# Layer 0 of a two-layer graph network: gathered rows in another column order, two harmonics weighted in one product, the parts summed by one reduce and one addition

## What is computed

```python
xs = x[:, :MUL_S]
xv = x[:, MUL_S:].reshape(n, MUL_V, 3)
...
out_s = (jnp.einsum('eu,uo->eo', xs_e * es[:, None], W_ss) / np.sqrt(MUL_S) + jnp.einsum('eud,ed,uo->eo', xv_e, ev, W_vv) * ISQ3 / np.sqrt(MUL_V)) * ISQ2
out_v = (jnp.einsum('eu,ed,uv->evd', xs_e, ev, W_sv) * ISQ3 / np.sqrt(MUL_S) + jnp.einsum('eud,e,uv->evd', xv_e, es, W_vs) * ISQ3 / np.sqrt(MUL_V)) * ISQ2
messages = jnp.concatenate([out_s, out_v.reshape(-1, 3 * MUL_V)], axis=1)
scale = jax.nn.sigmoid(edge_scalars @ W_rad.T + b_rad)
messages = messages * scale
agg = jax.ops.segment_sum(messages, dst, num_segments=n)
```

## Time and profile before

| | us |
|---|---|
| median of three runs | 4380.39 |
| profiled execution | 4373.24 |
| its span | 4371.4 |
| DVE busy | 3896.0 |
| PE busy | 3899.9 |
| POOL busy | 3139.9 |
| ACT busy | 2657.9 |

### The profile page before, as it was taken

The page is one execution under the profiler, slowest core; times in us unless marked ns, Lnnn a source line. Parts: engine busy times, 40 slices in busy tenths (PEclk is TensorE's granted clock), DMA queues, the critical chain, the costliest instruction groups (busy, mean ns, idle before and its releaser), DMA issues.

```text
span 4371.4 us, 64745 instructions
## 1 busy us (share of the span) xinstructions
PE 3899.9 (89%) x14024; PEld 2512.9 (57%) x14025; DVE 3896.0 (89%) x8569; ACT 2657.9 (61%) x8217; POOL 3139.9 (72%) x3268
## 2 busy tenths in 40 slices
PE   7899999989999998899878898899888898898887
PEld 5566666656666666666655555555555555555555
DVE  4999999999999999999768888998888998889987
ACT  5666666666666666666555566666656666566664
POOL 4777777777777777777457777777777777777771
PEclk7655555565555556655789999999999999999999
DMA  9666666666666666666333333333333333333331
GB/s 292 192 194 192 191 193 192 192 194 191 191 194 192 191 192 191 191 195 192 112 94 102 100 100 102 104 102 103 104 102 102 103 102 104 103 102 104 103 103 54
DMA packets 245745, 640.05 MB, mean 146 GB/s; under 512 B 57085, under 2 KB 95423, under 8 KB 245611
## 3 DMA queue, kind: packets, MB, share of 16 engines
q0 software_dynamic: 181136, 556.56, 46.4%
q1 hardware_dynamic: 64576, 83.11, 6.1%
HBM read 618.56 MB, written 20.88 MB: 146 GB/s over the span
## 4 chain that ended last, share of the span: by engine, by line
DVE 51%; PE 18%; issue 15%; DVEq 6%; DMA 4%; ACT 3%; POOL 2%; POOLq 0%; ACTq 0%; SPq 0%
PE ps L998 11%; DVE work L694 10%; DVE onehot L738 10%; DVE work L668 6%; DVE arena L746 4%; DVE work L718 3%; DVE work L661 3%; PE ps L975 3%; DMA arena<-table,srcs 3%; DVE work L681 2%; DVE work L715 2%; ACT work L480 2%; DVEq L803 2%; DVE acc L746 2%; POOL arena L383 2%
## 5 line engine op out<-in xcount | busy, mean ns | idle before, releaser
L383 POOL DMA_INDIRECT arena<-table,srcs x1596 | 1543.3, 967 | 486.4 <-issue 434.0
L383 POOL DMA_INDIRECT work<-table,srcs x1596 | 1526.1, 956 | 496.0 <-issue 479.8
L998 PE MATMUL ps<-work,onehot 128*128 128x384 f32 x3608 | 1310.8, 510 | 224.4 <-DVE work L725 129.2
L480 ACT ACTIVATE work<-arena,harm 128x160 f32<-128x160 f32 (+1 forms) x3224 | 985.4, 388 | 417.8 <-DMA arena<-table,srcs 400.5
L998 PE MATMUL ps<-arena,onehot 128*128 128x161 f32 x3608 | 1025.4, 461 | 183.2 <-DVE arena L704 156.2
L998 PEld LDWEIGHTS ps<-arena,onehot 128*128 128x128 f32 x3608 | 875.4, 305 | 501.6 <-issue 433.6
L480 ACT ACTIVATE work<-work,harm 128x96 f32<-128x96 f32 (+1 forms) x3224 | 1071.4, 415 | 131.1 <-DMA work<-table,srcs 73.7
L998 PEld LDWEIGHTS ps<-work,onehot 128*128 128x128 f32 x3608 | 670.9, 195 | 773.9 <-issue 325.4
L975 PE MATMUL ps<-wrad,escal 49*128 49x320 f32 x1612 | 899.8, 703 | 0.0
L738 DVE SCALAR_TENSOR_TENSOR onehot<-ps,bases,dst_sh 128x512 f32<-128x512 f32 x902 | 669.9, 743 | 14.6 <-DVE acc L746 7.3
L694 DVE TENSOR_REDUCE work<-work 128x256 f32<-128x768 f32 (+1 forms) x806 | 654.0, 850 | 1.5 <-ACT ps L508 1.0
(11 more groups left out here) (130 smaller groups left out, 2240.1 us busy)
## 6 DMA issues: line engine op xcount, KB each, us to landing
escal<-in_escal SPq DMA_DIRECT2D x404, 98.0 KB
arena<-table,srcs POOLq DMA_INDIRECT x1596, 3.5
work<-table,srcs POOLq DMA_INDIRECT x1596
table<-work SPq DMA_DIRECT2D x49, 224.0 KB, 5.9
dst_sh<-in_dst_sh SPq DMA_DIRECT2D x52, 160.0 KB, 3.2
table<-work SPq DMA_DIRECT2D x7, 784.0 KB, 4.0
acc<-in_xd SPq DMA_DIRECT2D x1, 3920.0 KB, 22.3
arena<-in_xd SPq DMA_DIRECT2D x7, 560.0 KB, 4.2
```

The lines of the kernel that those rows point to most:

```text
L383: pool.indirect_dma_start(out=rows[:, j, t, :], out_offset=None, in_=table, in_offset=bass.IndirectOffsetOnAxis(ap=of[:, j, t:t + 1], axis ...
L480: last = nc.scalar.activation(u[:, t, to:to + c1 - c0], r[:, t, c0:c1], ACT.Copy, scale=harm[:, j, at:at + 1])
L998: last = mm(bank(to)[:, 0:(MSG0, MSG1)[l]], onehot[:, b, t, :], m[:, j % 2, t, :], start=t == 0, stop=t == TPS - 1)
```

## The change

The table's columns, and with them the rows, are laid out anew, so that the two harmonics that DVE weights stand next to each other and all four parts of the scalars lie at the same distance in `weighted0`, as do the three components of the vectors. The rows of x are put in another order on the host for it. In the edge loop of layer 0:

- ACT weights columns 288 to 448 with harmonic 3 and 192 to 288 with harmonic 0, in eight instructions as before; the semaphore `s_whead` is gone.
- DVE copies the harmonics of a whole round into PSUM (`harm0`, bank 7), once a round, and makes one product for harmonics 1 and 2 over 128x768 elements, with the harmonics from PSUM, in place of the product of 384 elements and the four passes. It waits for the rows (`s_rows`) and not for ACT.
- It sums the four parts of the scalars in one reduce over 1024 elements, and the two parts of the vectors in one addition of 384 elements, in place of two reduces over 768 and 512 elements.

```diff
@@ weight_rows0
-                weight(u, r, 3, 96, 256, 128, j % PAIR).then_inc(s_whead, 1)
-                weight(u, r, 0, 256, 352, 288).then_inc(s_wtd[0], 1)
+                weight(u, r, 3, 288, 448, 64, j % PAIR)
+                weight(u, r, 0, 192, 288, 224).then_inc(s_wtd[0], 1)
@@ weight_by_one
                 if l == 0:
-                    dve.wait_ge(s_whead, s + 1)
+                    if j == 0:
+                        nc.vector.tensor_copy(harm0, of_round(i, slice(0, SLOTS), slice(TPS, 5 * TPS)).bitcast(f32)).then_inc(s_harmp[0], 1)
+                        dve.wait_ge(s_harmp[0], i + 1)
+                    dve.wait_ge(s_rows[0][j], (i + 1) * 16 * TPS)
                     u, r = weighted0[:, j % DEEP0, :, :], rows0[:, j, :, :]
-                    nc.vector.tensor_tensor(u[:, :, 384:480], r[:, :, 352:448], by(1), ALU.mult)
-                    for t in range(TPS):
-                        if t == 1:
-                            dve.wait_ge(s_add[0], s + 1)
-                        if t == TPS - 1 and not opens:
-                            dve.wait_ge(s_agg[0], s + 1)
-                        to = u[:, t, 128:224]
-                        last = nc.vector.scalar_tensor_tensor(to, r[:, t, 0:96], harm[:, j, 4 * t + 2:4 * t + 3], to,
-                                                              ALU.mult, ALU.add)
-                    last.then_inc(s_wone[0], 1)
+                    nc.vector.tensor_tensor(u[:, :, 320:512].rearrange("p t (k c) -> p t k c", k=2),
+                                            r[:, :, 0:192].rearrange("p t (k c) -> p t k c", k=2),
+                                            bc(harm0[:, j, :].rearrange("p (t k) -> p t k", k=4)[:, :, 1:3], 3, [P, TPS, 2, 96]),
+                                            ALU.mult).then_inc(s_wone[0], 1)
+                    if not opens:
+                        dve.wait_ge(s_agg[0], s + 1)
@@ messages0
-                summed(u[:, :, 0:MS], 160, 3)
+                dve.wait_ge(s_wtd[0], s + 1)
+                parts = u[:, :, 160:544].rearrange("p t (k c) -> p t k c", k=4)
+                nc.vector.tensor_reduce(u[:, :, 0:MS], parts[:, :, :, 0:MS].rearrange("p t k c -> p t c k"), AX.X, ALU.add)
                 dve.wait_ge(s_act[0], s + 1)
-                summed(u[:, :, MS:2 * MS], 224, 2).then_inc(s_part[0], 1)
+                vectors = u[:, :, MS:DIM].rearrange("p t (k c) -> p t k c", k=3)
+                nc.vector.tensor_tensor(vectors, vectors, u[:, :, 224:512].rearrange("p t (k c) -> p t k c", k=3)[:, :, :, 0:MV],
+                                        ALU.add).then_inc(s_part[0], 1)
@@ SCALED0: ACT scales w0a in two pieces in place of three; block.tensor: the second product of the table goes to other columns
-                mm(p[:, 32:128], x1[:, of_tile], w0b[:], start=False, stop=True).then_inc(s_tmm, 1)
+                mm(p[:, 224:320], x1[:, of_tile], w0b[:], start=False, stop=True).then_inc(s_tmm, 1)
```

More of the change, by code:

```diff
@@ L156, in mk_gnn_resnorm_d2_gnn_r8_694f30_kernel @@
         hps = bank(7)
+        harm0 = hps[:, 0:4 * TPS * SLOTS].rearrange("p (j c) -> p j c", j=SLOTS)
         half = [two_to_a_bank(2 * b, 224)[:, :, 192:] for b in range(2)]
@@ L438, in _ @@
             act.wait_ge(s_w0, 32)
-            for w, c in SCALED0[:3]:
+            for w, c in SCALED0[:2]:
                 nc.scalar.activation(w, w, ACT.Copy, scale=c).then_inc(s_w0scaled, 1)
@@ L616, in _ @@
                     dve.wait_ge(s_w0, 32)
-                    for w, c in SCALED0[3:]:
+                    for w, c in SCALED0[2:]:
                         nc.vector.tensor_scalar(w, w, c, None, ALU.mult).then_inc(s_w0scaled, 1)
@@ L1199 @@
     by_component = np.concatenate([s_of, *v_of])
+    v_of_kept = [MS + MV * d + np.arange(MV) for d in range(3)]
     xd = placed(NODES_PAD, DIM, (0, 0, x[:, by_component]))
@@ L1223 @@
     ins = {
-        "xT": xd.T, "xd": xd,
+        "xT": xd.T[np.concatenate([s_of, *(v_of_kept[d] for d in (1, 2, 0))])], "xd": xd,
         "srcs": np.concatenate([by_supertile(src, 0).transpose(1, 0, 2), np.zeros((P, SLOTS, TPS), src.dtype)], axis=1),
```

12 lines of the change are left out of this document (3 added, 9 removed).

## The result

| | before | changed |
|---|---|---|
| median of the runs, us | 4381.05 (4379.35 to 4384.94, 4 runs) | 4487.9 (4477.52 to 4491.06, 4 runs) |
| ratio, 95% interval | | 1.0239 (1.0227 to 1.0251) |
| span of the profiled execution, us | 4371.4 | 4489.2 |
| last gather of layer 0 starts at, us | 2107.7 | 2218.6 |

The forecast was 4363 us with a range of 4348 to 4390; 4487.9 lies 98 us above that range. The whole loss is in the edge loop of layer 0: its last gather starts 110.9 us later. From its first to its last gather, layer 1 takes 2036 us (2041 before).

What follows compares the result with a forecast made beforehand. It took POOL's gathers to pace layer 0, with DVE nearly tied. Gather surplus -32 us, new holds +16 and layer end -1 turned the profiled 4373.24 into 4356, or 4363 against the runs' median 4380.39; range 4348 to 4390.

Steps and rivals of the forecast that it cites:

- the price of the reduce: DVE, layer 0 edge loop: one reduce over 1024 elements taken at 1.29 us, 1.21 after overlap.
- a reduce well over 1.3 us: One of the listed signs that would show the prediction wrong, for the new DVE reduce in layer 0.
- fourth rival: No relief: with a big reduce of 1.7 us DVE keeps its 40.2 us, the layer its time; 4380 us, chance 0.07.
- the prediction's own sum for DVE: Layer 0, eight supertiles after the change: 8 x 4.29 + 2 x 1.14 + 1.1 = 37.7 us, below POOL's 40.06.
- The upper end of the range: 4390 us, taking in the blind-places rival (4375, chance 0.21) and part of the PE rival (4402, chance 0.06).
- POOL's bound and what DVE gives back: Layer 0: POOL's gathers set the pace; of DVE's 0.38 us saved a supertile only POOL's surplus returns, 32 us.
- the last message: End of layer 0: its start after the last gather falls from 10.74 to 9.7 us, - 1 us.
- the product's price and the addition's: DVE, layer 0: product of 128x768 at 0.87 us to the next start; addition of 384 elements 0.55, 0.59 with its wait.
- a gather which has started doesn't hold DVE: Layer 0: the addition runs its usual time inside a gather; rival, a lock in both directions, 4409 us, chance 0.01.
- The rival without stretches at full clock: PE at 1.2 GHz throughout needs 2072 us in layer 0, + 22 us; 4402 us, chance 0.06.
- the round: DVE, once a round in layer 0: 0.89 us of loop plus 0.25 for copy and wait, 1.14 us.
- the addition's place: Layer 0: the new addition falls mostly clear of gather starts, holding them 0.04 us a supertile, 16 us in all.

Runs made afterwards that it cites:

- four adjacent: Changed kernel, but the reduce sums four numbers lying side by side, not the four parts of one output, so its sums are others: 4350.63 us, ratio 0.9943.
- three parts: Changed kernel with the reduce over three of the four scalar parts, one left out of the sum: 4350.66 us, ratio 0.9928.
- three in PSUM, then one: Changed kernel with a reduce of three scalar parts into PSUM and an addition of the fourth in place of the four-part reduce: 4363.66 us, ratio 0.995.
- three in SBUF, then one: Changed kernel with a reduce of three scalar parts into SBUF and an addition of the fourth in place of the four-part reduce: 4376.89 us, ratio 0.9984.
- two additions: Changed kernel with the four scalar parts summed by additions of 512 and 256 elements, all inputs in SBUF, in place of the reduce: 4397.6 us, ratio 1.0037.
- two and three parts: Changed kernel with a three-part reduce, one part left out, and ahead of it an unread two-part reduce into PSUM: 4387.9 us, ratio 1.0006.
- three parts twice: Changed kernel with a three-part reduce, one part left out, and ahead of it an unread three-part reduce into PSUM: 4520.63 us, ratio 1.0327.

## Why the prediction was wrong, step by step

The second column adds the durations of what stands in the place of the scalar sum. In the kernel before it is both reduces, which do the vectors too; all others have the addition of 0.55 us for these beside it.

| kernel | sums, us | gathers in 200 to 1900 us | eight supertiles, us | mean gather there, ns | time, us | ratio |
|---|---|---|---|---|---|---|
| before | 1.70 | 1337 | 40.69 | 967 | 4381.1 | 1 |
| changed | 1.91 | 1263 | 43.07 | 952 | 4487.9 | 1.0239 |
| four adjacent | 1.21 | 1347 | 40.39 | 958 | 4350.6 | 0.9943 |
| three parts | 1.02 | 1351 | 40.27 | 954 | 4350.7 | 0.9928 |
| three in PSUM, then one | 1.46 | 1341 | 40.57 | 963 | 4363.7 | 0.995 |
| three in SBUF, then one | 1.45 | 1335 | 40.75 | 969 | 4376.9 | 0.9984 |
| two additions | 1.11 | 1318 | 41.27 | 986 | 4397.6 | 1.0037 |
| two and three parts | 1.72 | 1329 | 40.93 | 974 | 4387.9 | 1.0006 |
| three parts twice | 2.05 | 1243 | 43.77 | 945 | 4520.6 | 1.0327 |

- **The step that failed is the price of the reduce.** The prediction took 768 elements at 1.020 us and 512 at 0.681 and carried the line on to 1024, with ends of 1.28 and 1.36. Both rows are of sums whose parts are few enough; the third point of the line didn't exist. It took 1.906. The rows of before couldn't show this, but they did show that both known forms were other forms (two parts, three parts), and the bound should have been as wide as that. The prediction named "a reduce well over 1.3 us" as the sign of a mistake, and its fourth rival started from 1.7 us; it had 0.07.
- **What followed from it.** With 1.83 from start to start in place of 1.21, and 1.34 a round in place of 1.14, the prediction's own sum for DVE reads 37.7 + 8 x 0.62 + 2 x 0.20 = 43.06 us for eight supertiles. Measured: 43.07. The model of the two engines was right, and fed with the right price it gives the loss.
- **The rival that had a long reduce was mispriced, too.** It said that with a reduce of 1.7 us DVE would keep its 40.2 us and the layer its time, 4380. By the prediction's own sum a reduce of 1.7 us gives 37.7 + 8 x 0.41 = 41.0 us of DVE, already more than POOL's 40.7; 40.2 belongs to a reduce of 1.6. The kernel with 4.62 us a supertile, what a single reduce of 1.906 - (4.89 - 4.62) = 1.64 us would give, was at a ratio of 1.0006. There is no plateau behind that point. From there on each further us per eight supertiles costs 48 to 50, and the step to 1.9 is 102 us. The upper end of the range was set from cases in which DVE at most kept its time.
- **Right: POOL's bound and what DVE gives back.** With a reduce of 1.21 us (1.29 was assumed) the kernel takes 0.9943 of the time of before, the forecast was 0.9960 (4363 of 4380.39), just above the interval (0.9926 to 0.9959). The last gather moved by 13.3 us where 16 were predicted, and the last message followed it after 10.41 us (10.74 before) where 9.7 were. The rest of the gain lies elsewhere (see the end of this section), so the agreement of the total is in part luck.
- **Right: the product's price and the addition's**, and, in the main, that a gather which has started doesn't hold DVE: in no kernel did the additions take more than their usual time in the mean (543 to 554 ns for the 384 elements). Only those that started within some 0.05 us of a gather's start, on either side, were longer, by up to 0.08 us.
- **PE was not the bound.** The rival without stretches at full clock did not come in: the granted clock of the changed layer 0 was 0.56 (0.58 before), and DVE never waited for PE.
- **A size that was off: the round.** Copy, wait and loop cost 1.34 us where 1.14 stood (1.46 in the kernels that have one instruction more for the scalar sum); the copy was taken at 0.25 with its wait and needs 0.37 to the product's start. It is 0.4 us in eight supertiles; with the reduce at 1.29 us DVE would still have been below POOL's 40.06.
- **Partly right: the addition's place.** Between 600 and 1200 us it held 15 gathers of 120 supertiles in the kernel with three parts (DVE early, the predicted place mostly clear), but 40 of 119 with adjacent numbers and 42 of 118 with the sum in PSUM. At nearly the price that I had assumed, the place was nearly blind, at 0.06 us a supertile (7.0 us for 119) and not 0.04.

What stays open: the last gather of the four-adjacent kernel explains 13 us of its gain; the median is 27 below that of before. The profiled executions are 24 apart, and 9 of these lie in layer 1 (2031.9 us from first to last gather, 2041.0 before), whose instructions the change doesn't touch. The traces say where: POOL's few pauses there cost 9.6 us before and 4.4 in this kernel, and its gathers, 956 and 954 ns in the mean, make the other 4. Over the eleven kernels with the change layer 1 took 2027.9 to 2039.2 us. With one trace of each, chance isn't ruled out, and why the pauses differ isn't shown.

## What to carry to other kernels

An instruction's price can be carried along a line only within its form: before merging sums, ask how the addresses of one output lie, and price a new form of access by a form as far away as the doubt is, here the factor of 1.6 between 1.91 and 1.22 us. Where two engines run at nearly the same period, a saving on the one that is not the bound is worth only what it was costing the other, while every us that takes it past the meeting point is paid in full: the two sides of such a forecast are not alike. And an operand moved into PSUM can be worth more than a shorter instruction, if it lets go of something that another engine needs.

## What the runs showed of the hardware

- A reduce on DVE over four or more f32 parts at a distance: 1.91 us for 1024 elements to 256 outputs, 2.31 for 1280; the same 1024 side by side or 8 bytes apart, 1.22 (1.21 in the edge loop). Two and three parts at a distance: 0.70 and 1.04 us for 512 and 768, next to 0.69 and 0.95 side by side.
- The same in an addition: 256 elements with one input 16 or 32 bytes apart 0.61 us, at 4 or 8 bytes 0.43.
- An indirect gather of POOL that starts during a DVE addition with two SBUF inputs ends late by the rest of the addition less 0.13 us, unless the addition had started at most 0.045 us before it: then it often isn't held (87 of 139 times), and the addition takes up to 0.08 us longer. With one input in PSUM it isn't held either (43 gathers, 948 ns in the mean; 64 with both in SBUF, 1077): the addition took 425 ns in place of 427, and the mean gather 963 ns in place of 970.
